# Q, K and V biases moved into the last row of the weights, with that row's own values subtracted from the others

## The reference, cut to what matters

```
def _layernorm(x, axis=-1, eps=1e-05):
    m = jnp.mean(x, axis=axis, keepdims=True)
    v = jnp.var(x, axis=axis, keepdims=True)
    return (x - m) / jnp.sqrt(v + eps)

def proj(W, bias):                       # W is (128, 1024), bias (1024,)
    y = jnp.tanh(states @ W + bias)
    return y.reshape(b, s, h, d).transpose(0, 2, 1, 3)
q, k, v = (proj(Wq, bq), proj(Wk, bk), proj(Wv, bv))
alpha = jnp.einsum('bhqd,bhkd->bhqk', q, k) / jnp.sqrt(jnp.float32(d))
...                                      # causal mask, softmax
ctx = jnp.einsum('bhqk,bhkd->bhqd', alpha, v)
...
return jnp.tanh(ctx @ Wo + bo)

x = x + 0.5 * _L0_ffn_ref(_layernorm(x, axis=-1), gate_w, w1, b1, w2, b2)
x = x + _L0_attn_ref(_layernorm(x, axis=-1), Wq, bq, Wk, bk, Wv, bv, Wo, bo)
x = x + 0.5 * _L0_ffn_ref(_layernorm(x, axis=-1), gate_w, w1, b1, w2, b2)
```

## Time and profile before

| | |
|---|---|
| median of three runs | 452.63 us |
| the profiled execution | 452.66 us, its span (first to last instruction) 450.6 us |
| PE busy | 401.1 us (89%) |
| DVE busy | 321.7 us (71%) |
| ACT busy | 247.9 us (55%) |
| POOL busy | 207.6 us (46%) |
| chain that ended last | PE 63%, DVE 24%, issue 7%, POOL 2% |

### The profile page before, as it was taken

The page is one execution under the profiler, slowest core; times in us unless marked ns, Lnnn a source line. Parts: engine busy times, 40 slices in busy tenths (PEclk is TensorE's granted clock), DMA queues, the critical chain, the costliest instruction groups (busy, mean ns, idle before and its releaser), DMA issues.

```text
span 450.6 us, 11474 instructions
## 1 busy us (share of the span) xinstructions
PE 401.1 (89%) x4663; PEld 304.5 (68%) x4663; DVE 321.7 (71%) x856; ACT 247.9 (55%) x367; POOL 207.6 (46%) x176
## 2 busy tenths in 40 slices
PE   1589999678999999999999999999999989787992
PEld 0557677436777888587878587887678875555771
DVE  5788788526999977289898378789558888543321
ACT  2121564128768687477777377777468772133540
POOL 6566154255535534164434267453346541431446
PEclk9999999959999999999999999999999999999997
DMA  7912653127000000000000010000001100116531
GB/s 216 371 56 69 176 166 94 37 59 250 1 1 3 1 2 4 1 25 3 1 2 4 7 31 7 9 2 3 7 8 31 40 1 1 41 55 174 165 96 37
DMA packets 25372, 25.46 MB, mean 57 GB/s; under 512 B 2664, under 2 KB 21551, under 8 KB 25048
## 3 DMA queue, kind: packets, MB, share of 16 engines
q1 hardware_dynamic: 21424, 18.33, 13.7%
q0 software_dynamic: 2304, 4.25, 2.9%
q10 hardware_dynamic: 1592, 2.14, 1.3%
HBM read 16.72 MB, written 9.58 MB: 58 GB/s over the span
## 4 chain that ended last, share of the span: by engine, by line
PE 63%; DVE 24%; issue 7%; POOL 2%; ACT 1%; ACTq 1%; DMA 1%; POOLq 0%; DVEq 0%
PE sc L831 8%; DVE Pl L1344 7%; DVE Ph L1339 7%; PE sc L680 7%; PE pj L689 7%; PE pj L800 6%; PE tT L880 5%; PE cx L863 4%; PE cx L865 3%; PE cx L864 3%; PE pj L810 3%; PE tT L620 3%; PE pj L831 2%; PE pj L880 2%; PE sc L824 1%
## 5 line engine op out<-in xcount | busy, mean ns | idle before, releaser
L831 PE MATMUL sc<-Tq,Tk 64*128 64x128 f32 (+2 forms) x640 | 78.7, 345 | 0.0
L1339 DVE CAST Ph<-Pf 128x1024 f16<-128x1024 f32 (+1 forms) x48 | 49.8, 1038 | 31.0 <-ACT Pf L563 30.9
L863 PE MATMUL cx<-Vh,Ph 128*128 128x65 f16 x630 | 64.1, 195 | 8.8 <-DVE cn L1353 3.2
L831 PEld LDWEIGHTS sc<-Tq,Tk 64*128 64x128 f32 x640 | 62.4, 187 | 11.7 <-issue 0.2
L863 PEld LDWEIGHTS cx<-Vh,Ph 128*128 128x128 f16 x630 | 57.3, 97 | 15.6 <-DVE cn L1353 5.4
L864 PE MATMUL cx<-Vl,Ph 128*128 128x64 f16 x630 | 63.8, 193 | 0.0
L865 PE MATMUL cx<-Vh,Pl 128*128 128x65 f16 x630 | 63.6, 193 | 0.0
L864 PEld LDWEIGHTS cx<-Vl,Ph 128*128 128x128 f16 x630 | 57.7, 98 | 0.2
L865 PEld LDWEIGHTS cx<-Vh,Pl 128*128 128x128 f16 x630 | 57.8, 97 | 0.0
L481 ACT ACTIVATE hT<-sc,RT 128x320 f32<-128x320 f32 x64 | 33.8, 528 | 32.5 <-PE sc L680 31.9
L403 POOL TENSOR_TENSOR Vl<-Tv,Vh 128x512 f16<-128x512 f32 x16 | 19.6, 1223 | 66.8 <-ACT Vh L555 66.8
(11 more groups left out here) (251 smaller groups left out, 1052.9 us busy)
## 6 DMA issues: line engine op xcount, KB each, us to landing
W<-in_L_ffn_w SPq DMA_DIRECT2D x32, 256.0 KB, 2.9
disp<-empty SPq DMA_DIRECT2D x2, 1320.0 KB, 7.7
XE<-disp SPq DMA_DIRECT2D x18, 132.0 KB, 2.7
X<-xmid SPq DMA_DIRECT2D x4, 256.0 KB, 3.1
out<-X SPq DMA_DIRECT2D x4, 256.0 KB, 2.3
XR<-disp SPq DMA_DIRECT2D x18, 33.0 KB, 2.3
X<-in_L_attn_states SPq DMA_DIRECT2D x2, 256.0 KB, 3.3
X<-in_L_attn_states SPq DMA_DIRECT2D x1, 512.0 KB, 5.1
```

Source lines behind the costliest of these rows:

```text
L831: m = mm(score_bank(h, c)[:, o + x:o + y], Tk[u][half(h), q:q + P], Tq[u][half(h), q + x:q + y], start=False, stop=last and (c, h) != (2, 0))
L863: mm(bank[:, o:o + HD + 1], Ph[u][:, h, a:a + P], Vh[u][:, kt, h, :], start=kt == 0, stop=False)
L1339: dve.tensor_copy(Ph[u][:, :, at], Pf[u][:, :, at]).then_inc(S["p_hi"], 1)
```

## The change

Q, K and V lose their separate biases. Of each weight only the first 127 rows are loaded into the first 127 partitions of `Wf`. Later ACT issues for each weight two DMAs more: the bias into the last partition, and the weight's own row 127 read 127 times, once into each of 127 partitions of memory that `WH` and `WL` take up afterwards (`spread`). POOL waits for all ten DMAs and subtracts the spread row, in three instructions. The normalised x of the attention is written 127 columns wide, and its last column holds 1.0 from the start. `largest` now goes by weight, leaves Wo out, and moves from before the loop over experts into it, as the scale and the splits do (two splits at e = 2 and 3, one at 4 and 5).

```
+PARTS = {2: (0, 1), 3: (2, 3), 4: (4,), 5: (5,)}
...
+        spread = [WH[:, 0:2048].bitcast(F32), WH[:, 2048:4096].bitcast(F32), WL[:, 0:2048].bitcast(F32)]
+        LASTD = P - 1
... POOL
-            pool.memset(bvf[:], 0.0).then_inc(S["bv_zero"], 1)
-            pool.memset(bvs[:], 0.0).then_inc(S["bvs_zero"], 1)
+            pool.memset(xa[:, :, LASTD:P], 1.0)
...
             for k, (t0, tiles) in enumerate(FIRST):
                 dispatch(k, 0, t0, tiles)
+            pool.wait_ge(S["w_in"], 160)
+            for k in range(3):
+                part = Wf[0:LASTD, 1024 * k:1024 * (k + 1)]
+                pool.tensor_tensor(part, part, spread[k][0:LASTD, :], ALU.subtract).then_inc(S["folded"], 1)
             pool.wait_ge(S["amax"], 1)
             pool.partition_all_reduce(am[:, 1:2], am[:, 0:1], P, ABSMAX).then_inc(S["amax_all"], 1)
             experts(0)
... ACT
-            act.dma_start(rows[BQ_COL:BQ_COL + 8, :], bq.rearrange("(r p) -> r p", p=P)).then_inc(S["rows_in"], 16)
-            act.dma_start(rows[BK_COL:BK_COL + 8, :], bk.rearrange("(r p) -> r p", p=P)).then_inc(S["rows_in"], 16)
...
             for k, w in enumerate((wq, wk, wv)):
-                act.dma_start(Wf[:, 1024 * k:1024 * (k + 1)], w).then_inc(S["w_in"], 16)
+                act.dma_start(Wf[0:LASTD, 1024 * k:1024 * (k + 1)], w[0:LASTD, :]).then_inc(S["w_in"], 16)
...
             exp_logits(2, *FIRST[2])
-            for k in range(3):
-                if k == 0:
-                    act.wait_ge(S["bv_zero"], 1)
-                act.dma_start(bvf[32 * k:32 * k + 1, :], bv.rearrange("(a n) -> a n", a=1)).then_inc(S["bv_in"], 16)
+            for k, (w, bias) in enumerate(((wq, bq), (wk, bk), (wv, bv))):
+                act.dma_start(Wf[LASTD:P, 1024 * k:1024 * (k + 1)], bias.rearrange("(a n) -> a n", a=1)).then_inc(S["w_in"], 16)
+                act.dma_start(spread[k][0:LASTD, :], w[LASTD:P, :].broadcast_to([LASTD, 1024])).then_inc(S["w_in"], 16)
             experts(0)
...
-                act.activation(Tk[u][:], pj1[:], ACT.Tanh, bias=RT[:, BK_COL + r:BK_COL + r + 1], scale=unscale).then_inc(S["tk"], 1)
+                act.activation(Tk[u][:], pj1[:], ACT.Tanh, scale=unscale).then_inc(S["tk"], 1)
... PE (v); its waits for rows_in are 64 in place of 96, that for bv_ready is gone
-                        mm(o, (XL if xl else XH)[:, bass.ds(GN * b + P * t, P)], wpart(2, wl, r), start=k == 0, stop=False)
-                    last = mm(o, onesb[:], bvs[:, P * r:P * r + P], start=False, stop=True)
+                        last = mm(o, (XL if xl else XH)[:, bass.ds(GN * b + P * t, P)], wpart(2, wl, r), start=k == 0, stop=k == 2)
... DVE, experts(0): before the loop
-                    largest()
... in the loop over e; bias_high, bias_middle, bias_low and bias_rows are gone
-                    if e == 0 and between:
-                        between()
-                        if e < SPLITS:
-                            split_weights(e)
+                        if e == 0:
+                            largest(0)
+                            largest(1)
                         if e == 1:
+                            largest(2)
+                            largest_of_all()
                         if e == 2:
+                            between()
+                        for part in PARTS.get(e, ()):
+                            split_weights(part)
...
+            def largest(k):
+                dve.wait_ge(S["folded"], k + 1)
+                dve.tensor_reduce(amc[:, k:k + 1], Wf[:, 1024 * k:1024 * k + 1024], X_AXIS, ALU.max,
+                                  apply_absolute_value=True).then_inc(S["amax_part"], 1)
+            def largest_of_all():
+                dve.wait_ge(S["amax_part"], 3)
+                dve.tensor_reduce(am[:, 0:1], amc[:, 0:3], X_AXIS, ALU.max).then_inc(S["amax"], 1)
...
-                ln_apply(xa, GT * g, GT, S["xa_ready"], each=True)
+                ln_apply(xa, GT * g, GT, S["xa_ready"], each=True, width=LASTD)
```

More of the change, by code:

```diff
@@ L68 @@
 LATE, SPLITS = 5, 6
-B1_COL, BQ_COL, BK_COL, BO_COL, GW_COL, B2_COL, ROWS = 0, 32, 40, 48, 49, 57, 65
+PARTS = {2: (0, 1), 3: (2, 3), 4: (4,), 5: (5,)}
+B1_COL, BO_COL, GW_COL, B2_COL, ROWS = 0, 32, 33, 41, 49
 class Steps:
@@ L213, in macaron @@
         YH, YL = [Pl[0][:, k, 0:LATE * P].rearrange("p (b d) -> p b d", d=P) for k in range(2)]
-        names = """w_in rows_in bv_in slots_empty rows_kept consts bvs_zero bv_zero pool_const rt_ps rt_ready
+        names = """w_in rows_in slots_empty rows_kept consts pool_const rt_ps rt_ready
             carry0 stat_step scale_step var_ready rs_pow xn_ready xa_ready xa_ps xt_ps xt_ready
@@ L219, in macaron @@
             first_ready late_ready here_ready y_hi y_lo late_ps late_added
[L220 removed]
+            xm_ready order_ready spot_ready hot_ready n_hi n_lo part_in part_ps amax_part passed amax amax_all wscale folded w_split w_ready
             q_ps k_ps v_ps tq tk tv v_hi v_lo
@@ L540, in tanh_kq @@
                     act.wait_ge(S["s_ps"], 6 * (i - 1))
-                act.activation(Tk[u][:], pj1[:], ACT.Tanh, bias=RT[:, BK_COL + r:BK_COL + r + 1], scale=unscale).then_inc(S["tk"], 1)
+                act.activation(Tk[u][:], pj1[:], ACT.Tanh, scale=unscale).then_inc(S["tk"], 1)
                 act.wait_ge(S["q_ps"], i + 1)
-                act.activation(Tq[u][:], pj0[:], ACT.Tanh, bias=RT[:, BQ_COL + r:BQ_COL + r + 1], scale=unscale).then_inc(S["tq"], 1)
+                act.activation(Tq[u][:], pj0[:], ACT.Tanh, scale=unscale).then_inc(S["tq"], 1)
             def tanh_v(i, u):
@@ L739, in _ @@
             pe.wait_ge(S["consts"], 1)
-            pe.wait_ge(S["rows_in"], 96)
+            pe.wait_ge(S["rows_in"], 64)
             nc.tensor.transpose(pj0[:, 0:ROWS], rows[:], identf[0:ROWS, 0:ROWS]).then_inc(S["rt_ps"], 1)
@@ L1010, in ln_scale, with ln_apply @@
                 s.end()
-            def ln_apply(dst, first_tile, tiles, done, each=False):
+            def ln_apply(dst, first_tile, tiles, done, each=False, width=P):
                 for t in range(tiles):
                     row = X[:, first_tile + t, :]
-                    last = dve.tensor_scalar(dst[:, t, 0:P], row[:, 0:P], row[:, MEAN:RSTD], row[:, RSTD:ROW],
+                    last = dve.tensor_scalar(dst[:, t, 0:width], row[:, 0:width], row[:, MEAN:RSTD], row[:, RSTD:ROW],
                                              ALU.subtract, ALU.mult)
@@ L1273, in _ @@
             dve.memset(carry[:], 0.0).then_inc(S["carry0"], 1)
-            biases = Steps(dve, S["bv_ready"], 0, 8)
-            def bias_high():
-                dve.wait_ge(S["bv_in"], 48)
-                dve.wait_ge(S["bvs_zero"], 1)
-                biases.done(dve.tensor_scalar(bvr, bvf[:], am[:, 4:5], None, ALU.mult))
-                biases.done(dve.tensor_copy(bvt, bvr))
-            def bias_middle():
-                biases.done(dve.tensor_tensor(bvf[:], bvr, bvt, ALU.subtract))
-                biases.done(dve.tensor_copy(bvu, bvf[:]))
-            def bias_low():
-                biases.done(dve.tensor_tensor(bvr, bvf[:], bvu, ALU.subtract))
-            def bias_rows():
-                biases.done(dve.tensor_copy(bvs[0:32, :], bvt[0:32, :]))
-                biases.done(dve.tensor_copy(bvs[32:64, :], bvu[32:64, :]))
-                biases.done(dve.tensor_copy(bvs[64:96, :], bvr[64:96, :]))
-                biases.end()
-            def largest():
-                dve.wait_ge(S["w_in"], 64)
-                for k in range(4):
-                    last = dve.tensor_reduce(amc[:, k:k + 1], Wf[:, 1024 * k:1024 * k + 1024], X_AXIS, ALU.max, apply_absolute_value=True)
-                last.then_inc(S["amax_part"], 1)
-                dve.wait_ge(S["amax_part"], 1)
-                dve.tensor_reduce(am[:, 0:1], amc[:], X_AXIS, ALU.max).then_inc(S["amax"], 1)
+            def largest(k):
[5 more added lines that the diff above has]
+                dve.tensor_reduce(am[:, 0:1], amc[:, 0:3], X_AXIS, ALU.max).then_inc(S["amax"], 1)
             s = Steps(dve, S["wscale"], 0, 5)
```

10 lines of the change are left out of this document (removed).

## The result

The changed kernel takes **560.92 us** (median of 4 runs, 560.28 to 561.84), against 452.66 us of the kernel before on the same chip (4 runs, 449.5 to 453.99): ratio **1.242, interval 1.238 to 1.247**, slower by 108 us. The profiled executions stand at 560.79 and 452.66 us, with spans of 558.9 and 450.6 us; what follows explains the 108.3 us between the two spans.

What follows compares the result with a forecast made beforehand. PE was taken to bound most of the attention, with DVE late next. Profiled 452.7 + 104.7 delay of hidden(3) + 5.6 clock loss - 4.5 from the bias matmul = 558 us, range 522 to 605.

Steps and rivals of the forecast that it cites:

- One engine for 127 rows: ACT's queue: each of six 127-row transfers runs on one DMA engine, 123 us together; chance 0.86.
- The signs: Changed profile: one completion packet per transfer, DMA share near 0.06, first subtraction about 152 us, engines idle from 56, clock 0.50.
- The landing: Last spread row on the one engine: 6.5 + 123 + 1.9 + 16.6 + 4.1 = 152 us.
- It matters little when ACT issues the later three: Spread-row DMAs: their issue time hardly matters, since the one engine always has work; ACT's gap before 39.97 us would cover issuing.
- Never without work: The one DMA engine carrying the 127-row transfers: claimed to be busy throughout until the landing at 152 us.
- From landing to hidden(3): First experts: folds, reduce, outputs(0), rows and tokens(3) take 7.7 us, so PE goes on at about 159.7 us.
- The clock after the gap: PE after the idle wait: granted clock 0.50 once more, half of 11.24 busy us lost, 5.6 us added.
- The attention: V projection: removing bias matmul L811 gives 4.5 us, bounds 3 to 7.1; plain steps 7.23 in place of 7.45 us.
- Costed at nothing: Tanh without a bias operand and apply with 127 columns: worth 0, bounds ±0.5 us for the 16 applies.
- They would be hidden: POOL's three subtractions, 6.6 us: with weights there, they end by 49.5 us, ahead of DVE's e = 0 at 50.1.
- the second rival's number: No change: rows spread evenly, gain given back by the late all-reduce and by DVE in attention; 452 us, chance 0.03.
- the first's (447.6): Faster: rows spread over 16 engines, landed by 35 to 40 us, folds hidden; 445 to 451 us, chance 0.08.

Runs made afterwards that it cites:

- The half experiment: Changed kernel with weights loaded as 128 rows, ACT waiting for them before issuing the biases, spread rows still 127: 504.03 us, one run.
- lighter DVE: Kernel before with the larger of DVE's two subtractions per attention step replaced by writing zeros: 442.27 us, ratio 0.9776.
- 128-row version: Changed kernel with all six large transfers 128 rows high, ACT waiting for the four weights before issuing the biases: 451.03 us, ratio 1.001.

## Why the prediction was right, point by point

- **One engine for 127 rows** held, by the packets and by three experiments. The case given 0.86 is the one that came.
- **The signs** came in part. The share of one DMA engine in 16 is there (0.06 from 140 to 150 us), POOL's first subtraction came at 155.4 us for the 152 forecast, a 4096-byte row took 0.16 us (26 GB/s), and the clock was 0.50 after the gap. But PE, DVE and ACT were not idle from 56 us on: PE waited 55 us, until 65.3 us, worked, waited another 19.4 us for ACT's hT, until 116.6 us, and worked once more before the last gap. The forecast had the routing run at its old time.
- **The landing**: predicted 152 us, measured 155.4. Six transfers on one engine, from 7.0 us on, take 24.7 us of elapsed time each; (152 - 6.5)/6 is 24.3. Of the 0.9 us that two small DMAs less were to give, the first weight's issue shows 0.3 (7.03 for 7.31 us). The half experiment agrees: from 26.9 to 101.0 us three take 24.7 each. The sum of six at the row's price and of the engine's other work was the right form; the bounds with that work hidden in gaps (522) were not needed.
- **"It matters little when ACT issues the later three"** held for the last landing only, and there with luck: in the trace the packets of the weights end at 79.4 us and those of the spread rows begin at 81.5 us, so the engine stood for 2 us only. "Never without work" was close to untrue, and had ACT come any later, the landing would have moved with it. And the step saw one delay where there are two. ACT held in its issues is by itself worth some 53 of the 55 us of the half with 127-row weights, in which nobody waits for data. The two add up (106.5 us), since the spread rows can be issued only when ACT is through with the first half. The hold had been named only as a bound, up to 30 us on top; in fact it lies within the sum.
- **From landing to hidden(3)**: predicted 7.7 us (its terms add up to 7.6), measured 163.37 - 155.40 = 8.0.
- **The clock after the gap**: predicted 5.6 us, the term that was mis-sized on one side. hidden(3) took 3.99 us in place of 2.32, and everything up to the attention lost 1.9 us; the end of the kernel lost another 0.8 that may not be the clock. The row it was sized by, 13.7 us at 0.50, had PE waiting for others in part; half of a busy time is lost only if PE is the chain in it. Nor was PE idle from 82 to 92 us, ahead of that row: it was busy for 5.4 of the 10 us.
- **The attention**: predicted -4.5 us, the term mis-sized on the other side. The steps of after sum to -1.4 us, and the first step was 1.1 us shorter in these two traces, where the clock differed; -2.8 us in all by the marks. Right was the 0.22 us of a plain step (7.23 predicted and, without L811, measured; 7.17 after; 7.46 before). By L811 alone the forecast's parts were 0.5, 1.8, 1.1 and 1.1 us, and the four sequences gave about 0.4, 1.3, -0.2 and -0.1: what failed are the two where the chain changes hands. Wrong was to take L811's share of the chain as the gain: a removal also moves DVE's instructions against POOL's, and step 5 of these sequences pays 0.9 us. A bound below the given 3 us would have been needed.
- **Costed at nothing**: the tanh is not the same without its bias operand. The groups of ACT after, 32 of each (before 779 and 771 ns):
```profile
L543 ACT ACTIVATE Tq<-pj,am 128x512 f32<-128x512 f32 x32 | 22.0, 687 | 0.9 <-PE pj L800 0.9
L541 ACT ACTIVATE Tk<-pj,am 128x512 f32<-128x512 f32 x32 | 22.0, 687 | 32.0 <-PE pj L800 32.0
```
That is 5.6 us less of ACT. A plain step of after is 0.06 us shorter than one that only lacks L811 (7.17 and 7.23); that the tanh is the cause was not tested by itself.
- **"They would be hidden"**, of the three subtractions with 16 engines: they are not. They stand beside DVE's normalisations, and the tokens come late, about as much as L811 gives. So with 16 engines the second rival's number (452, no change) would have come and not the first's (447.6), but for another reason in the first place: the time was lost by hidden(2), ahead of the late all-reduce that the rival named (57.05 us; 48.80 before).
- The errors were +3.4 (landing), +0.3, -3.7 + 0.8 (clock and tail) and +1.7 (attention); together +2.5, against 560.8 - 558 = 2.8 (the sum is 558.5 before rounding). Without regard to sign they add up to 9.9 us, so that the total is closer than its terms is luck.

## What to carry to other kernels

Before a transfer is cut to 127 rows to keep one row free, count how many engines its row count can be dealt to; load 128 rows and overwrite the one behind a wait instead. Where a DMA issue lasts many times what its like took before (here 14 to 23 us for 0.5 to 1.3), the issuing engine's own work stands behind it: look at that engine as well as at whoever waits for the data. A line's share of the chain was an upper bound for what its removal gave in these kernels (4.5 and 1.2 us); where two other engines get in each other's way nearby, take a good part of it off.

## What the runs showed of the hardware

- A transfer of 127 rows left one mark of completion, one of 128 rows 16, and pieces of 100, 28, 126, 2, 120 and 8 rows left 63 together, the sum of their largest divisors up to 16. On one engine, 4096-byte rows move at 26 GB/s; ACT's instructions were held for 14.3, 22.7 and 19.7 us. How much a queue takes before it holds the engine was not measured.
- Beside a 127x1024 subtraction on POOL, two 128x128 instructions of DVE took 3.49 us for 0.6; beside the same subtraction on DVE, issuing a scatter took POOL 3.53 us for 0.96.
- A per-partition bias operand costs a 128x512 tanh 0.09 us (0.78 against 0.69).
- The mean granted clock from 89 to 107 us, about the start of the attention, was 0.62 to 1.00 from kernel to kernel (0.62 before and with a lighter DVE, 0.81 in the 128-row version, 0.91 with the subtractions on DVE, 1.00 with L811 twice or with extra matmuls). The first step of the attention took 5.27 us at 0.62, 4.18 at 0.81 and 3.13 at 1.00; of the last of these gains the third step took most back. One trace of each was read; how far the same kernel differs from run to run is not shown.
